# Key blocks and second-norm rows turned by VectorE and exchanged through DRAM instead of transposed on TensorE

## The chip, the core and the metric

The program runs on one core of one Trainium2 chip. The metric is the device time of one execution in microseconds. A core has TensorE (PE in the profile; its weight loads are PEld), VectorE (DVE), ScalarE (ACT), GpSimd (POOL) and SyncE (SP), each with its own instruction stream, joined by semaphores. All DMA transfers of this kernel are issued from SP and carried by the core's 16 DMA engines.

## What is computed

Two layers of cross attention and feed-forward over 8 batches of 128 tokens of width 512, all in float32:

```python
x = x + attention0(layernorm(x), ctx)          # one head, width 512
x = x + lora_ffn(layernorm(x))                 # dense 512x512, plus a LoRA of routed rank 8, 16, 32 or 64
x = x + attention1(layernorm(x), ctx)          # 32 query heads, 8 key heads of width 128
x = x + quantized_ffn(layernorm(x))            # 512 -> 1792 -> 512, silu gate
```

The parts that matter here are the keys of the second attention and the layer norm in front of the LoRA feed-forward:

```python
k = (ctx @ k_proj_w.T).reshape(B, KV, 8, 128)
k = k_norm_w * (k * rsqrt(mean(k * k, -1) + eps))      # per token and key head
q = q_norm_w * (q * rsqrt(mean(q * q, -1) + eps))
scores = q @ k.T / sqrt(128) + mask
xn = (x - mean(x)) / sqrt(var(x) + eps)                # feeds the dense product, the LoRA and the router
```

## The kernel before

The instruction order of every engine is written out by hand, and semaphores tie the streams together. A float32 product is made as three float32r matmuls of high and low parts (`three`, L1379 to L1383): high x high, high x low, low x high. One 128x512 tile is four contraction chunks, so twelve matmuls. PSUM is used as eight banks of 128x512.

The stage in question follows the first attention. `keys(m)` (L1441) makes the key block m, of 16: eight token tiles t for the key heads 0 to 3, then eight for the heads 4 to 7, in bank 6 + m % 2. ACT squares the block per head (`squares`, L754, called at L769), POOL adds epsilon and raises to -0.5 (`rms_of`, L544), DVE multiplies it into one half of `tb` (`key_norm`, L1093), PE transposes it in four 128x128 pieces against an identity (L1487), and ACT copies it with the scale `wqk` (product of the two norm weights) to `keyT`, the resident array that the attention loop reads (L776). The layer norm runs through the same loop: DVE normalises tile t (`ln_norm`, L1046), PE transposes it (`ln_transpose`, L1385, at L1478), ACT copies it twice from the bank, in float32 to `xnT32` (L719) and as high part to `xnT_hi` (L720), and DVE makes the low part (`ln_lo`, L1055). The PE loop at L1470 to L1488 runs over m from 2 to 17 and takes, in order, the key block m (for m of 16 and 17 a dense tile instead), a norm transpose and the transposes of key block m - 2.

After it come the routing and LoRA products (L1495), which read `xnT32`, then the remaining dense tiles, the routing chain on DVE, the values, and the attention loop of 64 steps. In that loop a query tile, and the probabilities, are already turned in another way: DVE transposes 32x32 blocks (L1195, L1189) into `tb`, SP writes them to the DRAM array `block_bounce` with four transfers (L464), one for each 32 partitions, and reads them back with one (L475) so that they land as a transposed tile in `land`; ACT copies from there to `headT` (L847), and PE multiplies `headT` with 128 columns of `keyT` (L1631).

SP's stream is in order: each transfer is issued when the semaphores in front of it have come. Up to the attention loop it holds loads alone (`load`, L416), each waiting for the low part of four chunks before it.

## Time and profile before

| | us |
|---|---|
| median of 3 runs | 874.53 |
| lowest, highest | 872.3, 875.42 |
| the profiled execution | 873.61 |
| its span | 871.8 |

| engine | busy us | share of the span |
|---|---|---|
| PE | 830.1 | 95% |
| PEld | 679.2 | 78% |
| DVE | 556.0 | 64% |
| ACT | 539.0 | 62% |
| POOL | 550.1 | 63% |

Busy time is that of instructions in execution; matmuls overlap each other, so the distance from one start to the next tells more of PE's pace than a record's length. The span starts with the first instruction and ends with the last; the profiled execution lasts 1.8 us more than its span. SP's instructions only issue transfers: their length is what the queue is held, and the time from issue to landing is told apart. The granted clock of PE was 0.995 in the mean.

### The profile page before, as it was taken

What the parts mean: (1) busy time and instruction counts of PE and PEld (TensorE: products, weight loads), DVE (VectorE), ACT (ScalarE), POOL (GpSimd) and SP (SyncE); (2) the same over time, 40 slices, a digit from 0 to 9 for tenths busy, and PEclk for the clock granted to TensorE, in tenths of its full rate; (3) what the DMA queues carried; (4) which work ended last, traced back from release to release, by engine and by line L of the source; (5) the groups of instructions that cost most, each with busy time, mean ns of one, the idle gap of its engine ahead of it and who ended that gap; (6) DMA issues with size and microseconds to landing.
All of it is one profiled execution on the core that took longest, in us unless ns stands there. A gap on an engine that the chain in (4) does not pass through costs nothing.

```text
span 871.8 us, 14112 instructions
## 1 busy us (share of the span) xinstructions
PE 830.1 (95%) x3984; PEld 679.2 (78%) x3984; DVE 556.0 (64%) x974; ACT 539.0 (62%) x1785; POOL 550.1 (63%) x557
## 2 busy tenths in 40 slices
PE   6899999999989999999999999999996899999995
PEld 5687888788878888888888888888885667777774
DVE  5505531432566666666666666666666799999996
ACT  4533672134677677767776677776674476767663
POOL 3332452212477777777777777777765368999985
PEclk9999999999999999999999999999999999999998
DMA  8511011003566666666667766667654023333302
GB/s 272 169 49 62 1 49 49 24 25 96 147 187 188 191 186 192 185 181 192 190 181 217 217 189 188 188 187 216 202 155 147 15 106 121 137 144 144 144 1 96
DMA packets 73224, 122.74 MB, mean 141 GB/s; under 512 B 8078, under 2 KB 45838, under 8 KB 73167
## 3 DMA queue, kind: packets, MB, share of 16 engines
q1 hardware_dynamic: 73166, 122.10, 46.4%
q8 instruction: 21, 0.34, 0.2%
q14 instruction: 37, 0.30, 0.1%
HBM read 86.41 MB, written 35.65 MB: 140 GB/s over the span
## 4 chain that ended last, share of the span: by engine, by line
PE 66%; DVE 15%; DMA 7%; ACT 4%; issue 3%; POOL 2%; SPq 2%; DVEq 0%; POOLq 0%; ACTq 0%
PE pair L1381 16%; PE pair L1383 16%; PE pair L1382 16%; PE pair L1537 5%; PE pair L1631 4%; DVE kv L1245 4%; DMA land<-block_bounce 4%; PE pair L1538 4%; DMA block_bounce<-tb 2%; DVE pair L1245 2%; DVE tb L1262 2%; ACT kv L943 2%; SPq L464 1%; ACT prob L872 1%; PE pair L1398 1%
## 5 line engine op out<-in xcount | busy, mean ns | idle before, releaser
L1381 PE MATMUL pair<-split,xnT_hi 128*128 128x512 f32 x288 | 114.2, 397 | 0.3 <-issue 0.3
L1382 PE MATMUL pair<-split,xnT_hi 128*128 128x512 f32 x288 | 112.1, 389 | 0.0
L1383 PE MATMUL pair<-split,xnT_lo 128*128 128x512 f32 x288 | 112.1, 389 | 0.0
L847 ACT ACTIVATE headT<-land 128x512 f32<-128x512 f32 x64 | 40.4, 632 | 100.8 <-DMA land<-block_bounce 87.5
L1381 PE MATMUL pair<-split,aoT_hi 128*128 128x512 f32 x256 | 100.2, 391 | 0.0
L1383 PE MATMUL pair<-split,aoT_lo 128*128 128x512 f32 x256 | 100.1, 391 | 0.0
L1382 PE MATMUL pair<-split,aoT_hi 128*128 128x512 f32 x256 | 100.1, 391 | 0.0
L872 ACT ACTIVATE prob<-pair,nmax 128x128 f32<-128x128 f32 x256 | 89.9, 362 | 13.5 <-DVE nmax L1209 13.3
L1537 PE MATMUL pair<-xnT_hi,split 128*128 128x512 f32 x224 | 89.5, 399 | 6.7 <-DVE tb L1262 3.2
L626 POOL TENSOR_TENSOR prob<-prob,rinv 128x512 f32<-128x512 f32 x64 | 66.6, 1041 | 37.1 <-DVE rinv L1179 37.0
L1538 PE MATMUL pair<-xnT_lo,split 128*128 128x512 f32 x224 | 87.4, 390 | 0.0
L1245 DVE SCALAR_TENSOR_TENSOR kv<-pair,gu_s,kv 128x1024 f32<-128x1024 f32 x65 | 83.4, 1282 | 4.9 <-ACT kv L943 0.4
L1179 DVE RECIPROCAL rinv<-rsum 128x4 f32<-128x4 f32 x64 | 11.4, 178 | 114.7 <-ACT prob L872 114.7
L650 POOL TENSOR_TENSOR probT_lo<-land,probT_hi 128x512 fp32r<-128x512 f32 x64 | 82.6, 1290 | 2.9 <-ACT probT_hi L865 2.3
L1203 DVE SCALAR_TENSOR_TENSOR pair<-pair,rms,mask_sb 128x128 f32<-128x128 f32 x256 | 72.1, 350 | 11.6 <-PE pair L1631 11.2
L1381 PE MATMUL pair<-split 128*128 128x512 f32 x160 | 67.0, 419 | 8.4 <-DVE split L1063 6.3
L617 POOL TENSOR_TENSOR split<-raw,split 128x512 fp32r<-128x512 f32 x55 | 70.9, 1289 | 2.2 <-ACT split L815 2.2
L1631 PEld LDWEIGHTS pair<-kv,headT 128*128 128x128 f32 x512 | 66.8, 191 | 6.1 <-ACT headT L847 1.2
L833 ACT ACTIVATE pair<-pair 128x128 f32<-128x128 f32 x256 | 70.1, 276 | 0.0
L1631 PE MATMUL pair<-kv,headT 128*128 (+1 forms) x512 | 67.4, 274 | 0.7 <-ACT headT L847 0.7
L636 POOL TENSOR_TENSOR rms<-msq,mhalf 128x4 f32<-128x4 f32 x64 | 64.4, 1007 | 5.3 <-POOL msq L632 0.5
L532 POOL TENSOR_TENSOR split<-raw,split 128x512 fp32r<-128x512 f32 x15 | 19.3, 1298 | 74.8 <-ACT split L712 74.7
(153 smaller groups left out, 2177.0 us busy)
## 6 DMA issues: line engine op xcount, KB each, us to landing
block_bounce<-tb SPq DMA_DIRECT2D x244, 128.0 KB, 2.3
land<-block_bounce SPq DMA_DIRECT2D x61, 512.0 KB, 3.5
raw<-in_wqo_dram SPq DMA_DIRECT2D x62, 256.0 KB, 3.1
kv<-in_ffn_w_dram SPq DMA_DIRECT2D x14, 768.0 KB, 4.4
kv<-in_ffn_z_dram SPq DMA_DIRECT2D x14, 768.0 KB, 5.6
resid<-in_x_dram SPq DMA_DIRECT2D x2, 1024.0 KB, 8.9
kv<-in_ctx_dram SPq DMA_DIRECT2D x1, 2048.0 KB, 9.4
out_dram<-resid SPq DMA_DIRECT2D x8, 256.0 KB, 2.3
```

The source lines that it names most:

```text
L617: pool.tensor_tensor(chunk_dst(WGRP + n, 1), raw[:, n % 2, :], as32(chunk_dst(WGRP + n, 0)), ALU.subtract).then_inc(s_lo, 1)
L650: pool.tensor_tensor(by_head(probT_lo[:]), landed(i + PLAG, 1), as32(by_head(probT_hi[:])), ALU.subtract).then_inc(s_ptl, 1)
L833: done = act.activation(bank[5][:, tile(h)], bank[i % 2][:, tile(h)], ACT.Square, accum_out=ssq[:, i % 2, h:h + 1])
L872: done = act.activation(prob[:, tile(h)], bank[2 + i % 2][:, tile(h)], ACT.Exp, bias=nmax[:, h:h + 1], accum_out=rsum[:, h:h + 1])
L1203: done = dve.scalar_tensor_tensor(out=cur, in0=cur, scalar=rms[:, i % 4, h:h + 1], in1=mask_sb[:], op0=ALU.mult, op1=ALU.add)
L1245: done = dve.scalar_tensor_tensor(out=cur if in_place else dst, in0=cur, scalar=scale, in1=acc, op0=ALU.mult, op1=ALU.add)
L1381: pe.matmul(dst, l_hi, r_hi, start=first, stop=False)
L1382: pe.matmul(dst, l_hi, r_lo, start=False, stop=False)
L1383: return pe.matmul(dst, l_lo, r_hi, start=False, stop=last)
L1537: pe.matmul(dst, w, r_hi, start=True, stop=False)
L1538: return pe.matmul(dst, w, r_lo, start=False, stop=True)
L1631: done = pe.matmul(bank[2 + i % 2][:, tile(h)], headT[:, tile(h)], keyT[:, bass.ds(g * TOK + t * P, P)], start=True, stop=True)
```

## The change

Neither key blocks nor the rows of the second layer norm are transposed on PE any more. Both take the way over DRAM that the queries take.

- Keys: DVE multiplies the block in place in its bank (`key_norm`), then transposes its 32x32 blocks into a half of `tb` (`key_turn`). SP writes it to `key_bounce` with four transfers of 32x4x128 and reads it back with two of 128x4x64, one for each pair of heads, straight into the resident array. There four pieces of 32 columns make the 128 columns of a head, which PE reads as such (`key_columns`). The scale `wqk` moves to the copy to `headT`.
- Norm rows: DVE transposes the 32x32 blocks of tile t into `score` or `prob` (`norm_turn`), SP writes four transfers to `norm_bounce` and reads one back into `xnT32(t)`. ACT and DVE make the high and low part from there (`landed_hi`, `landed_lo`), with a stride of four elements.
- Four banks hold key blocks in turn (6, 7, 4, 5) instead of two; PE's `keys(m)` waits for the turn of key m - 4. The first attention's second product uses the banks 2, 3, 0, 1.
- In front of the routing products PE waits for the turn of key 15.
- SP's loads of the value weights are put behind or between the new transfers.

```diff
+            def key_write(m):
+                sp.wait_ge(s_kt, m + 1)
+                if m >= 4:
+                    sp.wait_ge(s_kl[m % 2], 32 * (m // 2 - 1))
+                for quad in range(KT):
+                    sp.dma_start(key_scr[m % 4][:, :, quad, :].rearrange("d e c -> e d c"),
+                                 turned(m)[32 * quad:32 * (quad + 1), :].rearrange("e (d c) -> e d c", d=KT))\
+                        .then_inc(s_kw[m % 2], 16)
+            def key_read(m):
+                sp.wait_ge(s_kw[m % 2], 16 * KT * (m // 2 + 1))
+                for e in range(2):
+                    sp.dma_start(key_tile(m, e), key_scr[m % 4].rearrange("d e b c -> (d e) b c")[:, :, e * 64:(e + 1) * 64])\
+                        .then_inc(s_kl[m % 2], 16)
+            def norm_write(t):
+                sp.wait_ge(s_nt, t + 1)
...
+            def norm_read(t):
+                sp.wait_ge(s_nw[t % 2], 16 * KT * (t // 2 + 1))
+                sp.dma_start(xnT32(t), xn_scr[t % 4].rearrange("d e b c -> (d e) (b c)"))\
+                    .then_inc(s_nl[t % 2], 16)
+            key_write(0)
+            key_write(1)
+            key_read(0)
+            for m in range(3, 2 * T + 2):
+                if m <= 2 * T:
+                    key_write(m - 1)
+                if 3 <= m < 3 + T:
+                    norm_write(m - 3)
+                key_read(m - 2)
+                if 4 <= m < 4 + T:
+                    norm_read(m - 4)
+                if T + 4 <= m < T + 4 + KT:
+                    weights(WVAL + m - T - 4, WVAL + m - T - 3)
+            weights(WVAL + KT, WGRP)
...
@@ act
-            act.wait_ge(s_wqk, 1)
-            for m in range(2 * T + 2):
-                if m < 2 * T:
-                    act.wait_ge(s_ka, m + 1)
-                    if m >= 2:
-                        act.wait_ge(s_kr, m - 1)
-                    if m >= 1:
-                        act.wait_ge(s_ks, m)
-                    squares(bank[6 + m % 2], m % 2, s_ks)
-                if 5 <= m < 5 + T:
-                    ln_hi(1, m - 5, keep=True)
+            for m in range(2 * T):
+                act.wait_ge(s_ka, m + 1)
                 if m >= 2:
-                    n = m - 2
-                    act.wait_ge(s_kt, n + 1)
-                    g0 = REP * (n // T)
-                    act.activation(keyT.rearrange("p (g n) -> p g n", g=NKV)[:, g0:g0 + REP, tile(n % T)],
-                                   heads(bank[2 + n % 2][:]), ACT.Copy, scale=wqk[:, 0:1]).then_inc(s_ke, 1)
+                    act.wait_ge(s_kr, m - 1)
+                if m >= 1:
+                    act.wait_ge(s_ks, m)
+                squares(bank[KEY_BANK[m % 4]], m % 2, s_ks)
+                if 6 <= m < 6 + T:
+                    landed_hi(m - 6)
...
-                    act.activation(by_head(headT[:]), landed(i, 0), ACT.Copy).then_inc(s_qt, 1)
+                    if i == 0 and p is None:
+                        act.wait_ge(s_wqk, 1)
+                    act.activation(by_head(headT[:]), landed(i, 0), ACT.Copy, scale=wqk[:, 0:1]).then_inc(s_qt, 1)
...
@@ dve
             def key_norm(n):
                 dve.wait_ge(s_kr, n + 1)
+                cur = heads(bank[KEY_BANK[n % 4]][:])
+                dve.tensor_tensor(cur, cur, over(rms[:, n % 4, :], P), ALU.mult).then_inc(s_kn, 1)
+            def key_turn(n):
+                dve.wait_ge(s_kn, n + 1)
                 if n == 0:
                     dve.wait_ge(s_pt0, T)
                 if n >= 2:
-                    dve.wait_ge(s_kt, n - 1)
...
+                    dve.wait_ge(s_kw[n % 2], 16 * KT * (n // 2))
+                dve.transpose(by_block(turned(n)), split32(bank[KEY_BANK[n % 4]][:])).then_inc(s_kt, 1)
...
@@ pe
-                if m >= 2:
-                    pe.wait_ge(s_kn, m - 1)
+                if m >= len(KEY_BANK):
+                    pe.wait_ge(s_kt, m - len(KEY_BANK) + 1)
...
-            for m in range(2, 2 * T + 2):
-                if m < 2 * T:
-                    keys(m)
-                else:
-                    if m == 2 * T:
-                        lo_done(pe, WVAL - 1)
-                    dense(m - 2 * T)
-                if 4 <= m < 4 + T:
-                    ln_transpose(1, m - 4)
...
+            for m in range(2, 2 * T):
+                keys(m)
+            lo_done(pe, WVAL - 1)
+            pe.wait_ge(s_at0, T)
+            for t in range(2):
+                pe.wait_ge(s_xlo, T + t + 1)
+                dense(t)
             pe.wait_ge(s_lora, 32)
+            pe.wait_ge(s_kt, 2 * T)
             pe.wait_ge(s_xlo, 2 * T)
```

SP before, from the last key weights to the first transfers of the attention loop:

```order
L419 DMA land<-in_wkey_dram 128x512 x2
L440 DMA kv<-in_agT_dram 128x272
L441 DMA kv<-in_bTb_dram 65x512
L419 DMA raw<-in_wffn_dram 128x512 x2
L419 DMA land<-in_wffn_dram 128x512 x2
L419 DMA raw<-in_wval_dram 128x512 x2
L419 DMA land<-in_wval_dram 128x512 x2
```

SP after, from the dense weights (`in_wffn`) to the step of key block 4; lines are those of the changed kernel:

```order
L456 DMA raw<-in_wffn_dram 128x512 x2
L456 DMA land<-in_wffn_dram 128x512 x2
L491 DMA key_bounce<-tb 32x4x128 x8
L499 DMA kv<-key_bounce 128x4x64 x2
L491 DMA key_bounce<-tb 32x4x128 x4
L508 DMA norm_bounce<-land 32x4x128 x4
L499 DMA kv<-key_bounce 128x4x64 x2
L491 DMA key_bounce<-tb 32x4x128 x4
L508 DMA norm_bounce<-prob 32x4x128 x4
L499 DMA kv<-key_bounce 128x4x64 x2
L515 DMA kv<-norm_bounce 128x512
L491 DMA key_bounce<-tb 32x4x128 x4
```

The four rows ahead of the last are one step of SP's loop (m = 4), eleven transfers. Behind the dense weights stand now 136 transfers for 16 key blocks and 8 norm tiles, with the loads of the value weights behind the last norm read; before, those loads followed at once.

DVE before, three instructions for each key block in the middle of the stage, here around two blocks:

```order
L1058 TENSOR_TENSOR xnT_lo<-pair,xnT_hi 128x4x128 [waits ln_hi]
L1052 TENSOR_SCALAR headT<-resid,mv,rstd 128x512 [waits ln_transposed,ln_rstd]
L1099 TENSOR_TENSOR tb<-pair,rms 128x512 [waits key_transposed,key_rms]
L1058 TENSOR_TENSOR xnT_lo<-pair,xnT_hi 128x4x128 [waits ln_hi]
L1052 TENSOR_SCALAR land<-resid,mv,rstd 128x512 [waits ln_transposed,ln_rstd]
L1099 TENSOR_TENSOR tb<-pair,rms 128x512 [waits key_transposed,key_rms]
```

DVE after, five for each, in the middle of the stage:

```order
L1200 TENSOR_TENSOR pair<-pair,rms 128x512 [waits key_rms]
L1141 TENSOR_SCALAR headT<-resid,mv,rstd 128x512 [waits norm_blocks_turned,ln_rstd]
L1208 STREAM_TRANSPOSE tb<-pair 128x512 [waits key_blocks_written0,key_normed]
L1151 STREAM_TRANSPOSE land<-headT 128x4x4x32 [waits norm_blocks_written0,ln_normed]
L1156 TENSOR_TENSOR xnT_lo<-kv,xnT_hi 128x4x128 [waits ln_hi]
```

The semaphores of PE's transposes are gone from these waits; in their place stand those of SP's writes, two blocks back.

## Rows read from the trace of the kernel before

**Rows 1.** The page, first part: busy us (share of the span) and instructions.

```profile
PE 830.1 (95%) x3984; PEld 679.2 (78%) x3984; DVE 556.0 (64%) x974; ACT 539.0 (62%) x1785; POOL 550.1 (63%) x557
```

**Rows 2.** Timeline of PE: start us, length us, instruction, count [idle before it].

```profile
80.19 0.79 PE L1381 MATMUL pair<-split 128*128 128x512 f32 x1
...
88.01 0.50 PE L1381 MATMUL pair<-split 128*128 128x512 f32 x1 [0.89 <-DVE tb L1099]
...
98.97 0.47 PE L1381 MATMUL pair<-split 128*128 128x512 f32 x1
...
102.62 0.48 PE L1381 MATMUL pair<-split 128*128 128x512 f32 x1
...
136.54 7.26 PE L1495 MATMUL pair<-kv 128*128 128x68 f32 x64
...
171.14 0.39 PE L1381 MATMUL pair<-split 128*128 128x512 f32 x1
...
173.86 0.39 PE L1381 MATMUL pair<-split 128*128 128x512 f32 x1
```

**Rows 3.** Groups by line, 60 to 240 us; timelines of ACT and DVE.

```profile
L548 POOL TENSOR_TENSOR rms<-msq,mhalf 128x4 f32<-128x4 f32 x16 | 16.3, 1018 | 1.3
L776 ACT ACTIVATE kv<-pair,wqk 128x512 f32<-128x512 f32 x16 | 11.4, 714 | 4.4 <-PE pair L1487 4.4
L795 ACT ACTIVATE kv<-pair 128x512 f32<-128x512 f32 x16 | 9.6, 598 | 28.6 <-PE pair L1383 28.6
...
98.38 0.28 ACT L756 ACTIVATE land<-pair 128x128 f32<-128x128 f32 x1 [0.96 <-PE pair L1383]
...
87.27 0.69 DVE L1099 TENSOR_TENSOR tb<-pair,rms 128x512 f32<-128x512 f32 x1 [0.90 <-POOL rms L548]
...
111.43 0.69 DVE L1058 TENSOR_TENSOR xnT_lo<-pair,xnT_hi 128x512 fp32r<-128x512 f32 x1 [1.90 <-ACT xnT_hi L720]
...
112.49 0.68 DVE L1099 TENSOR_TENSOR tb<-pair,rms 128x512 f32<-128x512 f32 x1
```

**Rows 4.** Timeline of DVE: a turn out of PSUM and the next instruction.

```profile
210.93 0.72 DVE L1195 STREAM_TRANSPOSE tb<-pair 128x512 f32<-128x512 f32 x1 [4.72 <-PE pair L1383]
211.57 1.34 DVE L1169 TENSOR_TENSOR split<-raw,split 128x512 fp32r<-128x512 f32 x2
```

**Rows 5.** Timeline of SP; issue lengths by line, ns min/median/max; us to landing.

```profile
82.55 0.90 SPq L419 DMA_DIRECT2D land<-in_wffn_dram  x2
...
206.23 1.80 SPq L464 DMA_DIRECT2D block_bounce<-tb  x4
...
209.39 0.63 SPq L475 DMA_DIRECT2D land<-block_bounce  x1
...
214.79 0.53 SPq L475 DMA_DIRECT2D land<-block_bounce  x1
...
351.52 3.34 SPq L464 DMA_DIRECT2D block_bounce<-tb  x4
...
L464 SPq DMA_DIRECT2D block_bounce<-tb x268: 302/428/2019, 206.2 to 668.0; - x134
...
L475 SPq DMA_DIRECT2D land<-block_bounce x67: 326/338/626, 209.4 to 669.8; - x67
...
block_bounce<-tb SPq DMA_DIRECT2D x24, 64.0 KB, 1.8
```

**Rows 6.** PE's first matmul; a stretch near the end with its clock (after POOL).

```profile
6.25 0.77 PE L1381 MATMUL pair<-split 128*128 128x512 f32 x1 [6.25 <-DVE split L1063]
...
860.00:862.00 2.00, 2.00 (x6) 1.43 (x6) 1.50 (x2) 0.18 (x1) 2.00 (x2) 0.50 0.00 0
```

**Rows 7.** DMA of 211 to 214 and 8 to 16 us: packets, MB, share.

```profile
q1 hardware_dynamic: 978, 0.47, 57.6%
...
q1 hardware_dynamic: 1614, 3.11, 104.0%
```

**Rows 8.** The page's group of the score products: busy us, mean ns | idle before.

```profile
L1631 PE MATMUL pair<-kv,headT 128*128 (+1 forms) x512 | 67.4, 274 | 0.7 <-ACT headT L847 0.7
```

More of the change, by code:

```diff
@@ L430, in _, with weights @@
                 sp.dma_start(dst[:], src).then_inc(s_small, 16)
-            for c in range(WQ0, WGRP):
-                w, c0 = [(w, c0) for w, c0 in ((wq0, WQ0), (wkey, WKEY), (wffn, WFFN), (wval, WVAL))
-                         if c >= c0][-1]
-                load(c, w[c - c0])
+            def weights(first, end):
+                for c in range(first, end):
+                    w, c0 = [(w, c0) for w, c0 in ((wq0, WQ0), (wkey, WKEY), (wffn, WFFN), (wval, WVAL))
+                             if c >= c0][-1]
+                    load(c, w[c - c0])
+            for c in range(WQ0, WFFN + KT):
+                weights(c, c + 1)
                 if c == WKEY - 1:
```

119 lines of the change are left out of this document (82 added, 37 removed).

## The prediction, made before the changed kernel was timed

> **What bounds the kernel now.** I read the page first. TensorE (PE) is busy 95% of an 871.8 us span, the other engines 62 to 64% [rows 1], so work taken off PE is worth its full length wherever PE does not wait. The change takes it off one stage, the key stage, from 80.2 us (third key block) to 136.5 us (first routing product, L1495). The PE timeline there shows one wait, 0.89 us at 88.0; otherwise groups of twelve matmuls are laid end to end with the transposes between them [rows 2]. One group with both kinds of transpose runs from 98.97 to 102.62, 3.65 us. Twelve matmuls with nothing between (171.14 to 173.86) take 2.72 us [rows 2]. The stage is PE's own; DVE, ACT and POOL keep up. The SP queue issues ten loads in all of it.
>
> **What the change removes.** 64 key transposes and 32 transposes of the second layer norm leave PE. PE alone would need 14 key blocks and two dense tiles, 16 x 2.75 = 44.0 us from 80.2, and reach the routing products at 124.2 instead of 136.5: 12.3 us less, the 0.89 us wait included. On ACT sixteen key copies (0.71 us) and eight of sixteen norm copies go; they lay beside PE and were worth nothing [rows 3].
>
> **What it adds, engine by engine, in a step of one key block** (norm rows go along in eight of the steps):
> - DVE: multiply 0.62, norm rows 0.46, key turn 0.65, norm turn 0.63, low part 0.61 = 3.0 us, by the spacing of such instructions in the timeline (low part and norm rows 1.06 together, from 111.43 to 112.49; 0.64 from the turn at 210.93 to the next) [rows 3, 4]. PE's bare group takes 2.75, so DVE sits slightly above it.
> - ACT: four squares of 0.28 us [rows 3], about 1.1 with their accumulator reads, then one copy of a landed norm tile, 0.6 us: covered. The tile is read with a stride of four elements, which no row shows; were it twice as long, 2.3 us would still fit.
> - SP: four key writes, four norm writes, two key reads, one norm read, all from one in-order queue. In the first attention steps the same shape of write (32x4x128) takes SP 1.80 us for four, then 1.76 twice; a read cut into four pieces per partition takes 0.63 and 0.53, a whole one 0.34 [rows 5]. Over the whole run the 67 groups of four average 1.93 us (first 1.80, longest 3.34) [rows 5]. I take 1.85 for four writes, between the bare form and that mean, 0.53 for each half key read, 0.34 for a norm read and 0.04 between groups. The step then costs SP 2 x 1.89 + 1.14 + 0.38 = **5.3 us**, against 2.75 on PE now and 3.65 on PE before. Without norm rows it costs 3.0, with a value-weight load (0.33) 3.4.
>
> **Who waits for SP.** The key turn on DVE writes one of two halves of `tb`, and from key 2 on waits until the write of the key two before has landed; PE's product of key m waits for the turn of key m-4; ACT waits for norm tile m-6 before its next squares, and POOL and DVE wait for those squares. Behind that turn DVE has its norm turn and low parts queued. Before, DVE waited for PE's transposes alone; now the whole ring turns at SP's pace. And in front of the routing products PE waits for the turn of key 15.
>
> **The sum.** SP is free at 83.45, after the last dense-weight issue [rows 5]. Key 2 is turned at about 89.9: its multiply began at 87.27 [rows 3], two turns ahead of the loop, beside one gap of 0.54, put that about 0.9 later, and norm rows and turn follow. SP has by then written keys 0 and 1 and read key 0, and idles about 1.4 us. From there it never catches up. The turn of key 15 needs the write of key 13 landed. Ahead of that SP issues 14 key groups and 8 norm groups of writes (22 x 1.89 = 41.6), the two reads of twelve keys (12 x 1.14 = 13.7), eight norm reads (3.0) and two weight loads (0.7): 59.0 us. So it is issued at 83.5 + 1.4 + 59.0 = 143.9. A 64 KB write lands 1.8 us after its own issue began, 1.35 after that issue ended: 145.3. Turn 0.7, handover 0.1: PE starts the routing products at 146.1 instead of 136.5, **+9.6 us**. By the same count the write of key 9 is issued by 128.4, 15.5 us earlier. So the turn of key 11 is done at 130.5, the product of key 15 at 133.4 and the two dense tiles at 138.9, and PE then stands idle for 7 us. Nothing of the saving is left.
>
> The clock adds something. At the start PE had been idle for 6.25 us and its first record is 0.77 us long against 0.39 to 0.50 later on [rows 2, 6]; its first seven matmuls came 0.43 us apart instead of 0.23; near the end, behind further waits, a stretch of 2 us was granted 0.50, the 1.2 GHz level [rows 6]. Here PE has idled 7 us before the routing products, so I charge one such start, 7 x 0.20 = **+1.4 us**. In the key groups half clock would be nearly free: twelve matmuls at 0.43 are 5.2 us, no more than SP's step.
>
> After the routing products the order of work is the old one and PE's, so the delay should stay. The value-weight loads come later than before, but their high parts wait for the last key product, and the values are not begun before 168. In the attention loop SP's work is unchanged. The head copy on ACT gets a scale by a column; a PSUM copy with one takes 0.71 us, one without 0.60 [rows 3], so 0.1 x 64 = 6 us if it were bare. PE waited for that copy 0.7 us in all [rows 8] and so covers it; I put 0 and keep part in the range. So the total is +9.6 + 1.4 = +11.0 us: 873.61 + 11.0 = 884.6 for the profiled execution, and on the median, 874.53, which lies 0.9 above it, **885.5 us**.
>
> **Bounds of the main price.** Low: 1.77 for four writes and 0.34 for every read, whole or cut, no clock loss: 22 x 1.81 + 12 x 0.76 + 3.7 = 52.6, routing at 139.7, +3.1 us, 877.6. High: 1.93 and 0.63, two clock losses: 63.1, routing at 150.2, +13.6 + 2.8, 890.9.
>
> **Rivals.**
> *SP does not bound, the change is faster.* Should issues of the new transfers cost SP under about half of the rows, DVE and PE set the pace. Then only one stall is left: the multiply of key 4 waits for POOL, which first takes the reciprocal deviations of the second half (by the DVE steps above its statistics end near 95.5; add and power take POOL 1.3, twice) [rows 3], so key 8 starts 3.2 us late; DVE's 3.0 against 2.75 costs 0.9 more. Routing at 124.2 + 4.1 = 128.3, -8.2 us, **866.3 us**. It decides where the peak step falls below the old 3.65: two groups of four within 2.1 us, 0.27 us an issue. The shortest of 268 was 0.302, the median 0.428 [rows 5], and that speaks strongly against it. The Trainium skill (DMA: Bandwidth & Descriptors, section "Issuing engines are not separate DMA queues") says that issuing from several engines saves only the sequencer's time, "which is usually small relative to the DMA itself". By that rule this rival would win; the trace has four issues at 1.8 us beside a landing of 1.8. Chance 0.12.
>
> *SP is cheap but bounds.* The low bound above, about **878 us**, within the measurement. It needs cut reads as cheap as whole ones and no long groups. Chance 0.10.
>
> *The DMA engines bound, still slower.* A peak step moves 1,024 packets of 512 B, 1,024 of 256 B (the key reads) and 128 of 2 KB. In the stretch with 512 B traffic 978 packets took 57.6% of 16 engines over 3 us, 28 ns each; in the 2 KB stretch 1614 took 104% of 8 us, 82 ns [rows 7]. With 28 ns also for 256 B the step is 4.2 us of engine time, under SP's 5.3. With twice 28 for the short ones it is 6.0, and 5.1 in the steps without norm writes: 7 x 0.7 + 3 x 1.9 = +10.6 on top, **896 us**. No row shows a 256 B packet; I stay with 28. Chance 0.13. The Trainium skill (same page, section "Specifications") asks for at least 512 B per transfer for line rate and has smaller ones done as read-modify-write, which would point to this rival.
>
> *Scattered key columns slow the score products.* They now read 128 columns as four pieces of 32. The 512 records of that line are 67.4 us busy in all [rows 8], so each tenth more costs up to 6.7; a fifth gives 885.5 + 13.5 = **899 us**. No row shows PE streaming from such pieces, and nothing in the trace says that it slows. Chance 0.05.
>
> **How the numbers follow.** Forecast case, 880 to 891: 0.60. About 0.5% (4.4 us) is what a measurement of this kernel can tell from no change. Slower by more: 0.60 + 0.13 + 0.05 = 0.78; within: 0.10; faster: 0.12. The range runs from 878 to 897: it leaves out the faster case and the tails of the last two.
>
> **What would show it.** Right: in the key stage SP issues without a gap from 90 us on, at 5 to 5.5 us a step while norm rows run and 3 to 3.4 after; DVE's key turn waits for writes of the key bounce; PE waits for DVE 2 us and more at each key from the ninth; the routing products start at 143 to 150 us after a wait of 5 us or more, at half clock at first; the attention loop keeps its length. Wrong: four writes issued in 1 us or less; DMA share near 1 with landing times growing; or score products longer than their 274 ns [rows 8].

## The result, and the profile after

| | before | after |
|---|---|---|
| median | 874.59 us (4 runs, 872.3 to 875.42) | 908.58 us (4 runs, 905.5 to 912.04) |
| the profiled execution | 873.61 | 906.13 |
| its span | 871.8 | 904.1 |

The ratio is 1.0393, with a 95% interval from 1.0373 to 1.0413: slower, as forecast, but by 34 us where 11 were forecast, and above the range (878 to 897). The two profiled spans differ by 32.3 us. By the starts of the same instructions in both timelines they fall apart like this:

| stretch | before | after | longer by |
|---|---|---|---|
| to the first routing product | 136.54 | 152.73 | 16.2 |
| the routing products | 7.07 | 14.93 | 7.9 |
| the two dense tiles behind them | 5.55 | 6.58 | 1.0 |
| from there to the first bounce write of the attention loop | 57.1 | 57.1 | 0.0 |
| first to last bounce write (the loop) | 460.45 | 467.09 | 6.6 |
| the rest | | | 0.6 |

Timelines of PE, SP and DVE of the changed kernel, in the key stage and behind it (start us, length us, instruction [idle before it]):

```profile
123.15 0.50 PE L1495 MATMUL pair<-split 128*128 128x512 f32 x1 [3.06 <-DVE tb L1208]
129.48 0.80 PE L1495 MATMUL pair<-split 128*128 128x512 f32 x1 [3.29 <-DVE tb L1208]
...
142.15 0.53 PE L1495 MATMUL pair<-split,xnT_hi 128*128 128x512 f32 x1 [3.73 <-POOL split L622]
...
152.73 15.18 PE L1600 MATMUL pair<-kv 128*128 128x68 f32 x64 [3.26 <-issue]
167.66 0.77 PE L1495 MATMUL pair<-split,xnT_hi 128*128 128x512 f32 x1
...
174.24 1.04 PE L1611 MATMUL pair<-ident,kv 128*64 128x128 f32 x8
```

```profile
106.88 1.81 SPq L491 DMA_DIRECT2D key_bounce<-tb  x4
108.74 1.89 SPq L508 DMA_DIRECT2D norm_bounce<-prob  x4
110.67 1.20 SPq L499 DMA_DIRECT2D kv<-key_bounce  x2
111.92 0.62 SPq L515 DMA_DIRECT2D kv<-norm_bounce  x1
...
148.25 1.85 SPq L491 DMA_DIRECT2D key_bounce<-tb  x4
```

```profile
151.91 0.72 DVE L1208 STREAM_TRANSPOSE tb<-pair 128x512 f32<-128x512 f32 x1 [2.24 <-DMA key_bounce<-tb]
```

PE, which before had one wait of 0.89 us in this stage [rows 2], now stops in front of seven keys, 13.3 us in all. From 89 us on SP issues with 0.7 us of waits in all; a step of eleven issues (106.88 to 112.63) is 5.75 us, five of them in a row (106.88 to 136.59) take 5.9 us in the mean, and the later steps, without norm writes, 3.9. The write of key 13 is the row at 148.25, and the turn of key 15 waits for its landing. The waits of 80 to 153 us (us in total, times, longest) name the ring, the chain in which each engine waits for the next:

```profile
ACT xnT_hi L811 <- DMA kv<-norm_bounce: 26.7, 8, 4.5
...
PE pair L1495 <- DVE tb L1208: 13.3, 7, 3.3
...
DVE tb L1208 <- DMA key_bounce<-tb: 11.1, 8, 2.2
```

Groups of 60 to 200 us (busy us, mean ns of one | idle before), and two stretches by window (us, PE, PEld, DVE, ACT, POOL busy with counts, the granted clock, the DMA share, GB/s):

```profile
L1600 PEld LDWEIGHTS pair<-kv 128*128 128x128 f32 x64 | 15.0, 329 | 3.7 <-issue 3.7
L1156 DVE TENSOR_TENSOR xnT_lo<-kv,xnT_hi 128x512 fp32r<-128x512 f32 x8 | 10.2, 1270 | 0.0
L811 ACT ACTIVATE xnT_hi<-kv 128x512 fp32r<-128x512 f32 x8 | 8.9, 1115 | 26.7 <-DMA kv<-norm_bounce 26.7
L1151 DVE STREAM_TRANSPOSE prob<-headT 128x512 f32<-128x512 f32 x4 | 4.3, 1072 | 1.8 <-DMA norm_bounce<-prob 1.8
...
153.00:156.00 3.00, 3.00 (x14) 3.00 (x15) 0.00 (x0) 0.63 (x1) 0.82 (x1) 0.50 0.79 210
156.00:168.00 12.00, 12.00 (x53) 12.00 (x53) 0.56 (x3) 0.63 (x1) 1.72 (x2) 0.50 0.69 190
```

The routing products ran at the clock 0.50, the 1.2 GHz level, from end to end, and every operation that touches the norm rows in steps of four elements took half as long again to twice as long as its contiguous relative (a turn 0.72 us [rows 4], a low part 0.69 [rows 3]). In the attention loop the score products kept their 274 ns [rows 8]. What grew there are two stops of ACT, at the turns of its loop:

```profile
405.35 0.60 ACT L907 ACTIVATE aoT_hi<-pair 128x512 fp32r<-128x512 f32 x1 [4.46 <-issue]
520.94 0.60 ACT L907 ACTIVATE aoT_hi<-pair 128x512 fp32r<-128x512 f32 x1 [3.66 <-issue]
```

Before, the two had been 2.40 and 0.80 us. "Issue" means that the profile shows nothing that ACT waits for there.

### The profile page after: what moved, and what is told of

Read it like the earlier page. It is cut to its first block, busy times and chain, and to the rows that moved or that the text cites. A ratio compares the mean times of both kernels' runs of the same rounds, so it can differ in the third digit from the quotient of the medians.

```text
span 904.1 us, 14057 instructions
## 1 busy us (share of the span) xinstructions
PE 839.6 (93%) x3888; PEld 683.7 (76%) x3888; DVE 579.7 (64%) x998; ACT 538.7 (60%) x1761; POOL 553.6 (61%) x557
## 4 chain that ended last, share of the span: by engine, by line
PE 63%; DVE 14%; DMA 6%; SPq 6%; ACT 4%; issue 4%; POOL 2%; DVEq 0%; POOLq 0%; ACTq 0%
PE pair L1495 15%; PE pair L1497 15%; PE pair L1496 15%; PE pair L1641 5%; PE pair L1739 5%; PE pair L1642 4%; DVE kv L1359 4%; DMA land<-block_bounce 3%; ACT kv L1028 2%; DVE pair L1359 2%; PE pair L1600 2%; DVE tb L1376 2%; SPq L508 2%; DMA block_bounce<-tb 1%; SPq L491 1%
## 5 line engine op out<-in xcount | busy, mean ns | idle before, releaser
L932 ACT ACTIVATE headT<-land,wqk 128x512 f32<-128x512 f32 x64 | 46.3, 723 | 93.0 <-DMA land<-block_bounce 73.2
L1495 PE MATMUL pair<-split 128*128 128x512 f32 x160 | 68.3, 427 | 20.6 <-DVE tb L1208 13.3
L1495 PEld LDWEIGHTS pair<-split,xnT_hi 128*128 128x128 f32 x288 | 54.8, 190 | 17.2 <-POOL split L622 4.1
```

Source lines behind the costliest of these rows:

```text
L1495: pe.matmul(dst, l_hi, r_hi, start=first, stop=False)
```

## The experiments

All ratios below are to the kernel before, run beside it on the same chip. The medians come from several chips, on which the kernel before took 873.67 to 874.34 us; lengths of stretches are those of one profiled execution each. Each kernel computes what the reference asks for, unless its paragraph says otherwise.

### What doubled the routing products: stride or clock

**stride_warm**, the kernel before with the stride alone:

```diff
-        xnT32 = kv[:, 3 * QUART:4 * QUART].rearrange("p (m n) -> p m n", m=KT)
+        xnT32 = kv[:, 3 * QUART:4 * QUART].rearrange("p (n m) -> p m n", m=KT)
```

> The kernel before, but the float32 copy of the second norm (L127) is laid out so that the stationary operand of the routing products (L1495's kind, the 32 products of 68 columns) is read with a stride of four elements, as in the changed kernel; ACT's copy writes it with that stride. Nothing else moves, and TensorE is as busy ahead of the products as before. In the changed kernel these 32 products took 14.93 us against 7.07. Theory 'stride': the load of a strided stationary operand is what doubles them (its mean went from 192 to 329 ns); they take 15 us here too and the kernel 874.6 + 7.9 = 882.5. Theory 'clock': they are twice as long because the granted clock was 0.50 for them; here it stays at 1.00, they take 7.1 us and the kernel 874.6 to 876 (ACT's strided float32 copy may take about 1.1 us for 0.71, which its idle time covers).

**plain_cold**, the kernel before with idle time alone, in front of the routing products:

```diff
             pe.wait_ge(s_xlo, 2 * T)
+            lo_done(pe, WVAL + 3)
```

> The kernel before, with contiguous operands, but TensorE waits ahead of the routing products for the low part of the fourth value chunk, so that it stands idle there for some 5 to 8 us. Theory 'clock': after the idle stretch the granted clock is 0.50, the products take about 14 us for 7.07, the dense products behind them begin at half clock too (+1.0 in the changed kernel), and the kernel takes 874.6 + 6.5 (idle) + 7.9 + 1.0 = about 890. Theory 'stride': the products take 7 us at either clock, and only the idle time is added: 881.

Measured: stride_warm 884.56 us (1.0112, 1.0095 to 1.0129), plain_cold 888.92 us (1.0166, 1.0149 to 1.0183). Of stride_warm the products, its weight loads, and four stretches by window; of plain_cold the products and one stretch:

```profile
137.27 15.10 PE L1495 MATMUL pair<-kv 128*128 128x68 f32 x64
...
L1495 PEld LDWEIGHTS pair<-kv 128*128 128x128 f32 x64 | 15.0, 329 | 0.0
...
137.50:140.00 2.50, 2.50 (x12) 2.50 (x12) 0.00 (x0) 2.50 (x5) 1.24 (x2) 1.00 0.00 0
140.00:143.00 3.00, 3.00 (x14) 3.00 (x15) 0.00 (x0) 0.24 (x1) 3.00 (x4) 0.90 0.52 103
143.00:146.00 3.00, 3.00 (x15) 3.00 (x14) 0.51 (x2) 0.00 (x0) 0.71 (x1) 0.50 0.71 230
146.00:152.00 6.00, 6.00 (x28) 6.00 (x27) 0.00 (x0) 0.00 (x0) 0.00 (x0) 0.50 0.02 8
```

```profile
143.12 13.89 PE L1496 MATMUL pair<-kv 128*128 128x68 f32 x64 [6.40 <-POOL split L532]
...
144.00:156.00 12.00, 12.00 (x58) 12.00 (x58) 0.51 (x2) 0.00 (x0) 0.00 (x0) 0.50 0.09 29
```

Both theories were right about their own kernel and wrong to exclude the other. The stride alone doubles the products: they start at the clock 1.00 and pass at 12 in 2.5 us, and at 0.50 they pass at 15 in 3 us, the same pace; 14.9 us from the first to the next dense product. So with this operand strided the clock does not set the pace of the products; the strided operand is the one that the weight load reads. (The mean length of a load does not tell the two causes apart: it is 329 ns here and 332 in plain_cold, for 192 before.) Then, with PE recorded as busy all the time, the clock falls to 0.50 under them, and the two dense tiles behind them begin at half clock (7.4 us for 5.55). Idle time alone (6.4 us) doubles them as well: contiguous operands, clock 0.50, 13.6 us, and again 7.4 behind them. The fall of the clock is not a matter of DMA traffic: the share was 0.52 where it fell here, 0.81 where it stayed at 1.00 in dense_first below. Products and dense tiles together lost 9.6 us by the stride, 8.5 by the idle time's clock, and in the changed kernel, with both causes, 8.9: the cost of one of them, not of two.

The Trainium skill (SBUF — State Buffer, section "Door 1: The DMA port swizzle") says that SBUF has lines of 16 bytes, that at least two hits per line are needed for full bandwidth, and that each access which crosses to a new line pays. Four float32 elements are 16 bytes, so with this stride every access is to a new line. The same passage gives four float32 elements as the stride that is still free. The rows go with the first part and against the second: a stride of exactly four was not free, ACT's copy took 1115 ns, DVE's turn 1072, and the measurement decides. No other stride was run, so that the lines are the reason is argued, not shown.

**dense_first**, the changed kernel with more dense work between idle time and products:

```diff
-            for t in range(2):
+            for t in range(4):
                 pe.wait_ge(s_xlo, T + t + 1)
                 dense(t)
...
-            for t in range(2, HALF):
-                dense(t)
```

> The changed kernel, with the dense products of tiles 2 and 3 put ahead of the wait for the last key's turn and the routing products, instead of behind them. Of the two idle stretches of TensorE there (3.73 and 3.26 us) the second is filled. Theory 'clock': the products follow some 5 us of dense work instead of idle time; if that is enough to lift the clock, they take 7.1 us for 14.9, and the kernel takes 908.6 - 3.3 - 7.9 - 1.0 = about 896.5. Theory 'stride': they still take 15 us, and only the filled 3.3 us are won: 905.3. A third outcome, that the clock stays at 0.50 through dense work and products alike, would also give about 905, and the granted clock of the stretch tells it from 'stride'.

Measured: 909.57 us (1.0396, 1.0379 to 1.0413), no gain. The products started without a wait, and at full clock:

```profile
156.50:160.00 3.50, 3.50 (x17) 3.50 (x17) 0.00 (x0) 0.63 (x1) 1.11 (x2) 1.00 0.81 200
160.00:162.00 2.00, 2.00 (x11) 2.00 (x10) 0.00 (x0) 0.00 (x0) 0.89 (x1) 0.70 0.70 159
162.00:171.00 9.00, 9.00 (x40) 9.00 (x39) 0.51 (x2) 0.00 (x0) 0.00 (x0) 0.50 0.48 139
```

They took 15 us all the same and the clock fell again under them. The routing chain behind them now had no dense work beside it: PE waited 2.5 us for DVE, and its LoRA products (L1605, eight of them) took 7.2 us at the clock 0.50, for 3.7 in the changed kernel. What was filled in front was lost there, so the total fits none of the three expected outcomes, while the 15 us of the products at a clock that starts at 1.00 fit 'stride'.

**norm_pieces**, the changed kernel without the stride:

```diff
-                dve.transpose(xn_turned(t).rearrange("p (d a m) -> p d m a", d=KT, m=KT), split32_rows(ln_buf(1, t)))
+                dve.transpose(xn_turned(t).rearrange("p (d m a) -> p d m a", d=KT, m=KT), split32_rows(ln_buf(1, t)))
...
-                act.activation(xnT_hi[:, :, tile(t)], xnT32_by_row(t), ACT.Copy).then_inc(s_xhi, 1)
+                src = norm_land(t).rearrange("p (b m a) -> p m b a", b=KT, m=KT)
+                act.activation(blocks32(xnT32_by_row(t)), src, ACT.Copy)
+                act.activation(blocks32(xnT_hi[:, :, tile(t)]), src, ACT.Copy).then_inc(s_xhi, 1)
```

> The changed kernel without any access in steps of four elements: VectorE turns the norm's rows into blocks with rows of 32 adjacent elements, they land in free columns of kv, and ACT makes two copies a tile from there as in the kernel before (float32 contiguous for the routing products, and the high part). SP issues the same eleven DMAs a step. If the stride costs what it did in the kernel before (15.1 us of routing products for 7.1, then the clock at 0.50 behind them), the routing products take 7.1 to 14 us here, according to the granted clock when they start: TensorE still idles ahead of them, and after idle time alone contiguous ones took 13.9 us. So theory 'idle clock decides': about 13.9 us and 908.6 - 1 to -3 (VectorE's turn and low part and ACT's copy shorter by 0.4 to 0.6 us each) = 905 to 908. Theory 'stride decides': 7 to 8 us and 899 to 901.

Measured: 898.69 us (1.0289, 1.0262 to 1.0317).

```profile
154.20 13.45 PE L1611 MATMUL pair<-kv 128*128 128x68 f32 x64 [2.64 <-issue]
...
154.20:154.50 0.30, 0.30 (x3) 0.30 (x4) 0.00 (x0) 0.00 (x0) 0.04 (x1) 1.00 0.86 108
154.70:155.00 0.30, 0.30 (x4) 0.30 (x3) 0.00 (x0) 0.00 (x0) 0.00 (x0) 0.50 1.07 407
...
L822 ACT ACTIVATE xnT_hi<-kv 128x512 fp32r<-128x512 f32 x8 | 4.9, 613 | 0.0
L1162 DVE STREAM_TRANSPOSE land<-headT 128x512 f32<-128x512 f32 x4 | 2.8, 690 | 1.7 <-DMA norm_bounce<-land 1.7
```

In pieces of 32 the copy is back at 613 ns and the turn at 690. The products begin at the clock 1.00, behind 2.6 us of idle time, and fall to 0.50 within half a microsecond. They still take 13.2 us to the next start, and the dense tiles 7.6: "idle clock decides" held for them, and the stride's removal alone won 0.7 us in this stretch. They start 1.5 us later than in the changed kernel although ACT and DVE are faster, so these two did not pace the stage. The total fell further than it said, and not in the key stage: the attention loop took 460.1 us, not 467.1. That was not expected by either theory (905 to 908, or 899 to 901 with products of 7 to 8 us), and act_shift below follows it up.

### What paced the key stage: SP's issue time or the transfers

**reads_from_act**, the changed kernel with one edit, the reads of key blocks put from SP to ACT:

```diff
@@ sp
-                key_read(m - 2)
@@ act
                 squares(bank[KEY_BANK[m % 4]], m % 2, s_ks)
+                if m >= 4:
+                    key_read(m - 4)
```

> The changed kernel, with the 32 reads of key blocks issued by ACT instead of SP (by ACT at its step m the reads of key m - 4, the last four behind its loop; four landing semaphores for two). SP's list of a step is then nine issues for eleven: 1.20 us less of the 5.75 to 6.4 us that a step took. Theory 'issue': SP's time to issue bounds the stage; the steps shrink to some 4.6 to 5.2 us, the routing products start 8 to 13 us earlier than 152.7, and the kernel takes 895 to 900. Theory 'transfers': the 16 DMA engines with packets of 512 bytes and less bound it (67.9% busy there); moving the issue changes nothing, 907 to 910.

Measured: 895.46 us (1.0235, 1.021 to 1.026), 13.1 less than the changed kernel. SP's writes of one key follow each other like this, and the products start 9.3 us earlier:

```profile
104.16 2.06 SPq L491 DMA_DIRECT2D key_bounce<-tb  x4
...
108.95 1.83 SPq L491 DMA_DIRECT2D key_bounce<-tb  x4
...
113.30 1.98 SPq L491 DMA_DIRECT2D key_bounce<-tb  x4
...
118.76 1.88 SPq L491 DMA_DIRECT2D key_bounce<-tb  x4
```

```profile
143.47 15.17 PE L1602 MATMUL pair<-kv 128*128 128x68 f32 x64
```

Five steps from 104.16 to 128.02 take 4.8 us in the mean instead of 5.9, with the same transfers and packets. "Issue" held, "transfers" fell. The rule of the Trainium skill (DMA: Bandwidth & Descriptors, section "Issuing engines are not separate DMA queues") says that the sixteen DMA engines are shared whoever issues, and that the saved time of the sequencer is usually small relative to the DMA itself. That remark does not hold here: eleven issues of 0.45 to 0.62 us are the whole step. The price of an issue also depends on what the queue holds: a norm read behind two key reads took 0.62 us each time, and in mended_act below, with those on ACT, seven of eight took 0.38 to 0.46. The engines are not far behind as the next limit: their share was 0.92 in the mean of 130 to 144 us, against 0.67 to 0.80 in stretches of 4 us between 120 and 156 us with all issues on SP.

**one_read**, the changed kernel with one read of a key block for two. In this layout the first weights of the last feed-forward, which land in `kv` while attention runs, overwrite keys that are still to be read, so its scores are not the reference's; the instructions and their sizes are the same:

```diff
-                for e in range(2):
-                    sp.dma_start(key_tile(m, e), key_scr[m % 4].rearrange("d e b c -> (d e) b c")[:, :, e * 64:(e + 1) * 64])
+                sp.dma_start(key_tile(m, 0), key_scr[m % 4].rearrange("d e b c -> (d e) b c"))
```

> The changed kernel with one read of a key block for two: both key blocks' tiles are laid beside each other in kv (a tile's row of 32 numbers of four heads of either block), so that a key's read is one DMA with pieces of 512 bytes, and TensorE reads a head's columns in four pieces of 32 as before. SP's list of a step is ten issues for eleven. Theory 'SP's time to issue': a cut read took 0.60 us here and in pairs 1.20, so a step is 0.6 us shorter, the routing products start some 13 x 0.6 = 8 us before 152.7, and the kernel takes about 900. Theory 'number of packets': the gain is that or more, since the reads' packets double in size. If neither holds (the landing of a write sets the pace), the start stays within 2 us of 152.7.

Measured: 904.08 us (1.0348, 1.0328 to 1.0369). The products started at 146.25, 6.5 us earlier, where 8 were expected, so "SP's time to issue" held within 1.5 us and "number of packets", which asked for 8 or more, did not; 3.2 us of that were lost again in a longer attention loop (470.3 us).

### The loop

**scale_moved** and **keys_scattered**, the kernel before with the two parts of the change that reach into the attention loop:

```diff
-                                   heads(bank[2 + n % 2][:]), ACT.Copy, scale=wqk[:, 0:1]).then_inc(s_ke, 1)
+                                   heads(bank[2 + n % 2][:]), ACT.Copy).then_inc(s_ke, 1)
...
-                    act.activation(by_head(headT[:]), landed(i, 0), ACT.Copy).then_inc(s_qt, 1)
+                    act.activation(by_head(headT[:]), landed(i, 0), ACT.Copy, scale=wqk[:, 0:1]).then_inc(s_qt, 1)
```

> The kernel before, with one edit of the change alone: the scale wqk is no longer applied in ACT's copy of the key columns (L776) but in its copy of the query columns in the attention loop (L847 before). In the changed kernel the attention loop, from its first to its last bounce write, took 467.1 us against 460.5, and that copy 723 ns against 632. Theory 'scale': ACT's extra 0.09 us in each of 64 steps, and what it does where ACT has no slack (two loop edges), makes most of the 6.6: the loop takes 465 to 467 and the kernel 879 to 881. Theory 'not the scale' (the key columns in four pieces, or code ahead of the loop): the loop stays at 460.5 and the kernel at 874.5.

> As scale_moved, and also the key columns stored as the changed kernel stores them (two heads of a tile in a block, each head's 128 columns in four pieces of 32), written there by two ACT copies a tile for one. The key stage may grow by up to 16 x 0.2 us of ACT work, mostly beside TensorE. Theory 'pieces': the products that read them cost more in the loop than contiguous ones (a step 7.06 us for 7.03, and loop edges), so the loop is longer than that of scale_moved by 2 to 6 us. Theory 'no cost': both have the same loop within 0.5 us, since the profile of the changed kernel has 274 ns for these products as before.

Measured: scale_moved 874.50 us (1.0012, 0.9991 to 1.0033), loop 460.9 us, its copy 724 ns for 632; keys_scattered 876.55 us (1.0035, 1.0015 to 1.0054), loop 462.8, its score products 274 ns. So the scale is covered, as the prediction had it. For the pieces the answer is less clean: the loop is 2.0 us longer at unchanged products, and one of ACT's two stops is part of it (1.61 us for 1.03); the rest of the 2.0 is not explained.

**act_shift**, the changed kernel with eight one-element copies on ACT in the key stage, and **before_shift**, the same in the kernel before:

```diff
+                act.activation(kv[:, 3 * QUART - 8 + t:3 * QUART - 7 + t], xnT32(t)[:, 0:1], ACT.Copy)
```

> The changed kernel with eight more ACT instructions (a copy of one element a row, behind each copy of a landed norm tile), in time in which ACT is idle; nothing of the attention loop is touched. The loop took 467.1 us in the changed kernel and with the dense products first, 464.7 with the key reads issued by ACT, and 460.1 in norm_pieces, whose loop is the same but whose ACT has eight more instructions ahead of it. Theory 'place of the code': the gaps at the loop's two edges (4.46 and 3.66 us of ACT 'issue' in the changed kernel, 2.33 and 1.19 in norm_pieces) depend on where the loop's instructions lie; the loop is back at about 460 to 461 and the kernel at about 902. Theory 'not the place': the loop stays at 467 and the kernel at 908.

> The kernel before with eight more ACT instructions (a copy of one element a row) in the key stage, where ACT has idle time. The same edit took 4.7 us out of the attention loop of the changed kernel (467.1 to 462.4). Theory 'the place of ACT's loop code moves the gaps at the loop's edges': the loop here differs from 460.5 by 1 us or more, as likely up as down (gaps 2.40 and 0.80 us before), and the kernel with it. Rival 'only the changed kernel had something to lose': the loop stays at 460.5 within 0.5 us and the kernel at 874.

Measured: act_shift 900.52 us (1.0301, 1.0281 to 1.0321), 8.1 less than the changed kernel, with a loop of 462.4 us; before_shift 875.76 us (1.0024, 1.0009 to 1.0039), with a loop of 461.6 us and stops of 3.34 and 2.59 us for 2.40 and 0.80: 1.1 us more loop, just past the 1 us that was expected, for 2.7 us more of stops. The chain of waits at the first turn of the loop (start us, length us, what), of the changed kernel, of act_shift and of the kernel before:

```profile
400.89 2.14 issue
403.03 0.06 ACTq L985
403.16 2.19 issue
405.35 0.61 ACT aoT_hi L907
```

```profile
401.79 2.05 issue
403.83 0.06 ACTq L986
404.01 0.61 ACT aoT_hi L908
```

```profile
376.15 2.22 issue
378.37 0.06 ACTq L900
...
378.55 0.60 ACT aoT_hi L824
```

At this turn the stop is one piece of some 2.1 us before, two in the changed kernel, with next to nothing between them, and one again when eight instructions are put in far ahead. It is no fixed unit: before_shift has one piece of 3.15 us there. "Place of the code" held in its direction, with 462.4 where 460 to 461 was expected. Runs whose ACT stream is unchanged bear it out: dense_first and one_read, with that of the changed kernel, have loops of 467.1 and 470.3 us; stride_warm and plain_cold, with that of the kernel before, 460.6 and 459.6. That a piece is a fetch of instructions is argued, not shown: each of the two pieces of the changed kernel has one packet of the instruction queue in it, but such packets are also spread over stretches without a stop. The 8.1 us between the medians are more than the loop's 4.7; the profiled executions differ by 5.3, and the rest is not explained.

### The change repaired, and half of it

**mended** (with the layout of one_read, and the same remark on its scores) and **mended_act** (with the reads on ACT) both use the contiguous norm rows of norm_pieces, and wait in front of the routing products for the turn that their own banks need:

```diff
-            pe.wait_ge(s_kt, 2 * T)
+            pe.wait_ge(s_kt, 2 * T - 2)
             pe.wait_ge(s_xlo, 2 * T)
...
             pe.wait_ge(s_rt, 3 + NR + NR - 1)
+            pe.wait_ge(s_kt, 2 * T)
```

> The changed kernel with three edits: the norm rows in pieces of 32 and copied by ACT into a contiguous float32 array (norm_pieces), one read of a key block (one_read), and TensorE's wait ahead of the routing products for the turn of key 13 instead of key 15 (their banks hold keys 12 and 13; the wait for the last turn stands ahead of the transposes that use the banks of keys 14 and 15). By norm_pieces and one_read each alone: SP's step 0.6 us shorter, the routing products start at 140 to 146 for 152.7 (8 us from the read, 4 from the wait, less what the low parts of the dense weights then hold back), they take 7.3 to 13.5 us by the clock they find, and the kernel takes 885 to 892. If the clock is at 1.00 when they start, the lower end.

> The changed kernel with its key reads issued by ACT (reads_from_act), the norm rows in pieces of 32 and copied into a contiguous array (norm_pieces), and TensorE's wait ahead of the routing products for key 13's turn only. reads_from_act had the products start at about 143.5 and take 15 us; by the other two edits they start at 140 to 143 and take 7.3 us if TensorE's idle time ahead of them is gone, 13.5 if not. Loop 460 to 467 by the place of its code. So 874.3 + 5 + 0 to 6 = 879 to 885 if the products run at the clock 1.00, 886 to 892 at 0.50.

Measured: mended 881.98 us (1.0091, 1.0072 to 1.0111); mended_act 882.65 us (1.0090, 1.0062 to 1.0117). The products of the two:

```profile
144.86 7.25 PE L1610 MATMUL pair<-kv 128*128 128x68 f32 x64
```

```profile
142.07 7.25 PE L1613 MATMUL pair<-kv 128*128 128x68 f32 x64
```

Without stride and without idle time in front they take 7.25 us again, in both; mended came out below its range of 885 to 892. Of the 34 us, some 26 are gone; what is left in mended_act is the later start (5.5 us), a wait of 1.2 us for the routing chain, and a loop 2.9 us longer than before.

**keys_only**, the changed kernel with the norm rows turned on PE and copied by ACT as before:

```diff
-                if 3 <= m < 3 + T:
-                    norm_write(m - 3)
...
-                if 4 <= m < 4 + T:
-                    norm_read(m - 4)
...
             for m in range(2, 2 * T):
                 keys(m)
+                if 4 <= m < 4 + T:
+                    ln_transpose(1, m - 4)
```

> The changed kernel with the second norm's rows turned on TensorE and copied by ACT as before; only the key blocks go through DRAM. SP then issues six DMAs a key (4 x 0.46 + 2 x 0.60 = 3.05 us) for eleven (5.8). TensorE needs 2.78 us for a key's products and 0.35 to 0.44 for a norm tile's transposes, so SP and TensorE are about even at 3.1 us. Theory 'issue bounds the stage': the routing products start at 131 to 136 us for 152.7 (136.5 before), stay at full clock with 7.1 us, and the kernel takes 874.6 - 3 + 6.6 (the attention loop as in the changed kernel) = 876 to 881. Theory 'latency bounds it' (write, landing and read of a key, not the number of issues): the steps stay above 4 us, the start is 145 or later and the kernel takes 890 or more.

**keys_best** adds one_read's layout (same remark), the earlier wait of mended, and the norm transposes a step later; **keys_early** is keys_best with the two reads of the changed kernel:

> keys_only with one read of a key block, the wait ahead of the routing products for key 13's turn, and TensorE's first norm transpose a step later (in keys_only it stood idle 3.36 us there, and 1.24 us ahead of the routing products, where they started at 135.34). SP issues five DMAs a key, 1.85 + 0.6 = 2.5 us, below TensorE's 2.8 to 3.2. Theory: TensorE bounds the stage again and without gaps, the start is at 131 to 133 and the kernel takes 869 to 872 in all its executions; keys_only's executions fell at 871.5 to 873.8 and at 877 to 880.5, with mean granted clocks of 0.993 to 0.995 and of 0.983 to 0.988, and the longer ones should be gone. Rival: the longer executions come from elsewhere (the attention loop) and stay.

> keys_only with two of the three edits of keys_best: the wait for key 13's turn and the first norm transpose a step later, and with two reads a key as in the changed kernel. keys_best took 869.8 with one read, start of the routing products at 134.57. SP needs 3.05 us a key here, TensorE 2.8 to 3.2, and 3.7 from key 12 on, where the value weights' loads join; the wait for key 13's turn hides these. Theory: start at 134.5 to 136, products 7.25 us at the clock 1.00 in all executions, kernel 869 to 873. Rival: SP's 3.05 us leave TensorE idle in gaps, the clock falls in some executions as in keys_only (877 to 880), and the median is 874 to 878.

Measured: keys_only 877.30 us (1.0032, 1.0005 to 1.0058), its ten executions spread from 871.5 to 880.5; keys_best 869.82 us (0.9953, 0.9937 to 0.9969); keys_early 870.24 us (0.9953, 0.9935 to 0.9970), six executions within 869.3 and 871.2. The first routing products of keys_only and keys_early, and the latter's first norm transposes:

```profile
135.34 7.33 PE L1594 MATMUL pair<-kv 128*128 128x68 f32 x64 [1.24 <-issue]
```

```profile
101.85 0.65 PE L1502 MATMUL pair<-ident,headT 128*128 128x128 f32 x4 [3.77 <-DVE xnT_lo L1154]
...
133.54 7.25 PE L1594 MATMUL pair<-kv 128*128 128x68 f32 x64
```

Without the norm rows on the way over DRAM some 31 of the 34 us are gone. With these off SP's list, its six issues cost 3.05 us a key, PE's work 2.8 to 3.2. In keys_early PE has one wait between 84 and 147 us, the 3.77 us above, so PE paces it again, and the key half of the change, with the two further edits, is worth 3 to 4 us. keys_early is the version that beats both kernels: 0.5% faster than before. The spread of keys_only is gone in both kernels that have no gap in front of the routing products; its longer executions had a mean granted clock of 0.983 to 0.988, its shorter ones of 0.993 to 0.995, but which stretch ran at half clock in the longer ones was not profiled. One read for two (keys_best) gained nothing more: SP waited 10.0 us for DVE's turns there between 84 and 134 us, 2.9 in keys_early, so it no longer paces the stage. The wait of 3.8 us ahead of the first norm transpose moved with the transpose instead of going, and PE keeps 3.0 of the 12.3 us that were taken off it.

## Why the prediction was right or wrong

The profiled spans differ by 32.3 us where 11.0 were forecast. The missing 21.3 are 6.6 in SP's list, 7.5 in the routing products and the dense tiles behind them (8.9 for the 1.4 of the clock term), 6.6 in the attention loop and 0.6 elsewhere. The mechanism of the first term was right and its size off; the clock term and the unchanged loop were wrong as steps.

- **Direction and bound: right.** SP's one queue paced the stage, DVE's turn waited for it, PE waited for DVE, and the steps were predicted at 5.3 us with norm rows and 3.0 to 3.4 without; they took 5.9 in the mean and 3.9 (the latter with a norm read or a value load in each). reads_from_act shows it by taking 1.2 us off a step. The rival that the DMA engines bound is refuted by the same run, and "SP does not bound" by every row of SP.
- **SP's list: the term was mis-sized.** The write of key 13 was issued by 150.1 instead of 143.9. In pure issue time 63.4 us stand against 56.8 by the prediction's terms: the 24 halves of key reads 14.7 for 12.7 (0.60 each and more, not 0.53), the eight norm reads 5.0 for 2.7 (0.62, not the 0.34 of a whole read in an empty queue), two value loads 1.2 for 0.7, the 22 groups of writes 42.5 for 40.7. The upper bound for a read, 0.63 [rows 5], was near the true price for all of them in this kernel; the prediction's own high sum, 63.1, used it for the key reads and left the norm reads at 0.34. The landing of key 13 took 0.45 us longer than charged; start, idle time and gaps came to 0.4 less. Together that is the 6.6 us by which 16.2 exceeds 9.6.
- **The clock term: the step that failed.** "I charge one such start, 7 x 0.20 = +1.4 us" took the start of a stream of full matmuls ([rows 6]: seven at the slower pace, then the faster one) as a model for 64 short ones, under which the clock did not come back. plain_cold shows what idle time costs there: 6.6 us in the products and 1.9 behind them.
- **The stride: not priced at all for PE.** The prediction saw the stride of four elements on ACT alone ("were it twice as long, 2.3 us would still fit"; it was twice as long, and it fitted). It did not ask who else reads that array. stride_warm puts 7.8 us on the products and 1.8 on what follows. Since stride and clock cost about the same on the same products, the changed kernel lost 7.9 + 1.0 and not the sum. Removing the idle time alone (dense_first) recovered nothing and removing the stride alone (norm_pieces) 0.7; with both gone (mended_act) the products are back at 7.25.
- **DVE's step: wrong size, no effect.** 3.0 us were forecast; the strided turn (1.07) and low part (1.27) make it about 1.1 longer. It stays under SP's step.
- **The idle time in front of the products: 3.3 us, not 7**, because POOL delivered the last low part of the dense weights late and PE waited 3.7 us there first. The clock was lost all the same.
- **The attention loop: "keeps its length" failed by 6.6 us.** The two reasons considered, scale and scattered columns, were rightly held small: 0.4 us, and at most 2.0. The rest goes with ACT's stops at the loop's turns, 4.9 us more than before, though before_shift shows that a longer stop need not lengthen the loop as much. No part of the change aims at them and no row of before could price them; the trace of before did show the stops themselves, as 2.40 and 0.80 us of "issue".

## What to carry to other kernels

Price an issue by the row of its own shape in a full queue, not by the cheapest relative, and count issues per step before counting bytes. When the layout of an array changes, list every reader of it, PE's stationary side above all, and look at what short matmuls do to the clock: where two causes each double the same stretch, an experiment that takes away only one shows nearly nothing (0.7 us here). Wait for what the next instruction needs (the turn of key 13), not for the end of the stage; and when a loop grows that nobody touched, compare the stops at its turns before explaining it.

## What the runs showed of the hardware beyond what was expected

- A stationary operand read in steps of four float32 elements: 12 products in 2.5 us at the clock 1.00, 15 in 3 us at 0.50, against 7.07 us for all 64 when contiguous (stride_warm, before). ACT's copy 1115 ns for 613, DVE's turn 1072 for 690, its low part 1270 for 785.
- The granted clock can fall from 1.00 to 0.50 while PE is recorded as busy without a gap: in stride_warm from 140 to 143 us, in dense_first from 160 to 162, both times some microseconds into the strided products. Contiguous ones kept 1.00 when PE had been busy ahead of them or idle for 1.24 us (before, mended, keys_only). Behind 2.64 us of idle time they began at 1.00 and fell to 0.50 within half a microsecond (norm_pieces), behind 6.4 us they began at 0.50 (plain_cold), and in both they stayed there for 13 us.
- ACT stopped at the turns of its loop, in pieces of 2.05 to 3.15 us at the first one, and eight instructions hundreds of microseconds earlier changed their number and length: loops of 467.1 and 462.4 us, and of 460.5 and 461.6 us.
